# Attention on strips of the TensorE array: scores by row strips, values by column strips

## The chip, the cores and the metric

The kernel runs on one core of one Trainium2 chip. The metric is the device time of one execution in microseconds. Before the change three runs took 1524.38, 1525.86 and 1531.93 us; the median is 1525.86 us.

## What is computed

One layer over x of 4 x 2048 tokens with 512 features: a cross attention with 16 heads of 32 features over 77 context rows per batch, added to x, and then a mixture of 8 experts, top 2 of 8 with a capacity of 1024 tokens, added again.

```python
x = x + xattn(layernorm(x), ctx_768, Wq, bq, Wk, bk, Wv, bv, Wo, bo)
x = x + ffn(layernorm(x), expert_embeddings, first_linear, second_linear)

# xattn: heads H=16, D=32, scale D**-0.5
q = (query @ Wq + bq)        # [B, 16, 2048, 32]
k = (key_value @ Wk + bk)    # [B, 16, 77, 32]
v = (key_value @ Wv + bv)
attn = softmax(clip(einsum('bhqd,bhkd->bhqk', q, k) * scale, -1e4, 1e4))
x = einsum('bhqk,bhkd->bqhd', attn, v).reshape(B, Nq, Cq) @ Wo + bo

# ffn: router weights = softmax over the top 2 of 8 logits; each expert takes up to 1024 tokens
inter = relu(einsum('ech,eih->eci', tokens, first_linear))
out = einsum('eci,ehi->ech', inter, second_linear) * vals[:, :, None]
```

## The kernel before

The 8192 tokens are 64 tiles of 128. The kernel has two stages: attention with the router, and then the experts (from about 830 us on, not touched by the change). In attention the layernorm, scores, softmax and residual go tile by tile (index t); the query projection, the values product and their copies go by groups of two tiles (index G, 32 groups, 256 tokens, `GW` = 256).

Every product of the attention in 16 bits is made of three matmuls: operands are split into a high and a low half in fp16, and high x high, high x low and low x high are summed in PSUM. "g" is a head group of four heads, that is 128 of the 512 features.

The steps of the attention that the change and the prediction touch:

- `tx`, L601: PE transposes the normalised tile (fp32) into bank T; ACT copies the high half (L608), DVE makes the low half (L614).
- `q_mm`, L634: per G and g, 12 matmuls of 256 columns. ACT reads the bank twice (`halves`, L650): once as fp16 into `qT`, once as fp32 into `part`; POOL subtracts (`low`, L655) and gets the low half. `part` has four slots, which q and o share in turn.
- `s_mm`, L670: scores of tile t and head group g: 3 matmuls of 308 columns (4 heads x 77 keys). The stationary operand is q of 128 features x 128 tokens, and the keys stand block-diagonal in `kb`, three quarters of them zero. The four head groups have four PSUM banks, in two halves (S0, S1): a half is free once DVE has written `sd` from it.
- DVE per half: row maxima (`s_max`, L688 and L691), then subtraction into `sd` (`s_sub`, L695). ACT: Relu L703, Exp L707. DVE: sums L713. POOL normalises (L726), ACT casts (L731), POOL makes the low half (L735), and SP transposes both halves by DMA into `pT` (L740).
- `pv_mm`, L752: values, per G and g. The 16 x 77 = 1232 rows of keys lie in 10 chunks of 128. A head group touches 3 or 4 chunks; each is 3 matmuls of 128 x 128 against 256 columns, 39 in all per G. Each head group takes a PSUM bank of the pair A, uses 256 of its 512 columns, and is read by ACT twice (L651) and by POOL once (L655).
- `o_mm`, L773: output projection, 12 matmuls of 512 columns per tile. DVE adds the residual (L780). `t2`, L796: PE transposes the result, ACT copies it into `x1T` (L802, two buffers), `logits`, L827: 4 matmuls of 8 columns in fp32, each of which the trace shows as two.
- `put`, L1006 on POOL, `pick`, L991 on ACT and `invert`, L1017 on PE build the table of tokens per expert.

The banks A (two) serve `q_mm`, `pv_mm` and `o_mm` in turn. The order of instructions on each engine isn't the order of the code: a planner in the kernel keeps a clock per engine, and at each step takes the stage that can start in the earliest slot of 0.3 us by its table of costs, ties going by the table `RANK`. What stands in each engine's queue is fixed by that when the program is built; on the chip each engine works its queue in order and waits on semaphores.

Of the kernel before, what the change touches and what calls it, by code (L numbers as in the profile page):

```python
# [6 lines left out]
F32 = mybir.dt.float32  # L7
# [37 lines left out]
    "place1": 3.0, "values_max": 6.18, "values_split": 9.0, "values_place": 21.39, "output_max": 22.0,  # L45
    "output_split": 28.0, "factors": 9.28, "out_factor": 29.0, "keys_mm": -3.12, "keys_bias": -2.8,
    "values_mm": 4.1, "values_copy": 11.32, "emb_center": 20.48, "zero_v": -1.93, "numbers": 31.0,
    "ln1_stats": -6.54, "rsqrt1": 17.94, "ln1_apply": 18.24, "add_bo": 22.74, "tx": -4.11, "tx_hi": 26.0,
    "tx_lo": 19.9, "q_mm": 29.38, "q_hi": -27.75, "q_lo": 37.39, "s_mm": 47.47, "s_max": 82.86, "s_sum": 78.49,
    "p_norm": 80.36, "p_hi": 80.45, "p_lo": 24.82, "p_T": 105.11, "pv_mm": 101.04, "o_hi": 82.88, "o_lo": 72.54,  # L50
    "o_mm": 72.59, "residual": 94.24, "t2": 108.61, "t2_copy": 106.55, "logits": 130.25, "choose": 126.29,
    "choose2": 100.97, "rsqrt2": 83.51, "gates_of": 142.27, "rank": 156.16, "rank2": 141.44, "onehot": 194.91,
    "value": 184.83, "invert": 184.01, "load_w1": 300.0, "load_w2": 300.0, "prep": 400.0, "s_sub": 64.76,
    "s_min": 66.71, "s_exp": 72.85, "load_x": 70.23, "load_s": 12.21, "store_o": 84.42, "store_x": 74.15,
# [3 lines left out]
    "tx_lo": 0.65, "q_mm": 1.4, "q_hi": 0.87, "q_lo": 0.76, "s_mm": 0.42, "s_max": 0.45, "s_sub": 0.9, "s_min": 1.32, "s_exp": 1.32,  # L58
    "s_sum": 0.75, "p_norm": 2.28, "p_hi": 1.2, "p_lo": 2.5, "p_T": 2.8,
    "pv_mm": 1.15, "o_hi": 0.78, "o_lo": 0.76, "o_mm": 2.7, "residual": 0.0, "t2": 0.5, "t2_copy": 0.6,  # L60
# [90 lines left out]
def xattn_moe(nc, x, ctxT, wq, bq, wk, bk, wv, bv, wo, bo, embT, w1T, w2T, out, xrow):  # L151
    ctx = ExitStack()
    with ctx:
# [62 lines left out]
        part = sb("part", [P, 4, GW], F32)  # L216
# [3 lines left out]
        x1T = sb("x1T", [P, 2, 4, P], F32)  # L220
# [109 lines left out]
        dma("sp", lambda e: e.dma_start(wof[:, :, :], wo.rearrange("(c p) n -> p c n", p=P)), ("l_wo",))  # L330
# [149 lines left out]

        pieces = [(n, c, h, max(NKV * h, P * c), min(NKV * (h + 1), P * (c + 1))) for n, (g, c) in enumerate(PAIRS)
# [17 lines left out]
        def output_max():  # L499
            amax(3, flat3(wof[:, :, :]), [("l_wo",), ("s_z", 0)], ("a_o",))  # L500
            yield
            reduce_max(3, "sco", ("a_o",))
# [964 lines left out]
```

How the kernel before makes its waits and increments, by code:

```python
    def run(self, name, eng, sems):  # L141
        for item in self.queues[name]:
            if item[0] == "wait":
                eng.wait_ge(sems[item[1]], item[2])
            else:
                ins = item[1](eng)
                if item[2] is not None:
                    ins.then_inc(sems[item[2]], item[3])
```

## Time and profile before

| what | value |
| --- | --- |
| median of three runs | 1525.86 us |
| the profiled execution's own time | 1524.85 us |
| its span | 1523.1 us |
| PE busy | 1411.5 us |
| DVE busy | 982.1 us |
| POOL busy | 857.8 us |
| ACT busy | 825.6 us |
| `s_mm` (L670), matmuls, busy | 768, 129.7 us |
| `pv_mm` (L752), matmuls, busy | 1248, 161.5 us |

PE is TensorE's matmuls, PEld its weight loads, DVE is VectorE, ACT ScalarE, POOL GpSimd, SP the queue that issues most DMAs. The ends of matmuls are modelled: a matmul's length in the trace includes its way through the array, so that the next one starts before it ends. What a run of matmuls costs is read from the start of the run to the start of the next one.

### The profile page before, as it was taken

Reading aid. Unit: us, or ns where it says so; the run is one execution under the profiler, and the core shown is the slowest. Engines: PE = TensorE matmul, PEld = TensorE weight load, DVE = VectorE, ACT = ScalarE, POOL = GpSimd, SP = SyncE. Lnnn points to the kernel's source line nnn. Section 1 sums busy time; section 2 is a strip of 40 time slices with the busy share of each in tenths; the row PEclk is TensorE's granted clock in tenths of the full one; section 3 lists DMA queues with packets and bytes.
Section 4 is the critical chain, followed back from the end, with each engine's and each line's share of the span. In section 5 each row is a group of like instructions: output and inputs, shape, how many; then the busy total and the mean of one; then the engine's idle time right before and its main releaser. Section 6 shows DMA issues by size and latency. Waiting matters only on the chain.

```text
span 1523.1 us, 23892 instructions
## 1 busy us (share of the span) xinstructions
PE 1411.5 (93%) x8807; PEld 875.2 (57%) x8807; DVE 982.1 (64%) x1950; ACT 825.6 (54%) x1472; POOL 857.8 (56%) x907
## 2 busy tenths in 40 slices
PE   6787999989998999999964899999999999999996
PEld 2565777768776777768743644444444444444442
DVE  7895898978877877787766454545454555545430
ACT  4675787668886888768854451504233342425120
POOL 2596788879997899878966414232232414151301
PEclk9898999999999999999976999999999999999998
DMA  6166877568664655746734347465556556474401
GB/s 227 47 154 141 187 200 175 128 143 209 149 145 92 150 122 129 191 102 148 187 93 142 98 129 182 128 171 149 149 164 159 161 127 165 125 196 116 114 14 42
DMA packets 312062, 215.09 MB, mean 141 GB/s; under 512 B 252345, under 2 KB 252729, under 8 KB 311946
## 3 DMA queue, kind: packets, MB, share of 16 engines
q1 hardware_dynamic: 295411, 162.84, 43.6%
q0 software_dynamic: 15360, 50.66, 11.3%
q8 instruction: 70, 1.15, 0.3%
q14 instruction: 46, 0.38, 0.1%
q10 hardware_dynamic: 1175, 0.07, 0.1%
HBM read 105.62 MB, written 50.86 MB: 103 GB/s over the span
## 4 chain that ended last, share of the span: by engine, by line
PE 79%; DVE 5%; SPq 4%; POOL 4%; ACT 3%; issue 2%; DMA 2%; ACTq 1%; DVEq 0%; POOLq 0%
PE ps L1314 22%; PE ps L1335 22%; PE ps L634 9%; PE ps L773 7%; PE ps L752 7%; PE ps L670 5%; SPq L494 3%; PE ps L827 2%; PE ps L601 2%; POOL put L1006 1%; PE ps L796 1%; POOL ph L735 1%; DMA pT<-ph 1%; PE ps L464 1%; DMA wvf<-wv 1%
## 5 line engine op out<-in xcount | busy, mean ns | idle before, releaser
L1314 PE MATMUL ps<-xT,w1s 128*128 128x512 f16 (+1 forms) x1632 | 335.2, 368 | 0.0
L1335 PE MATMUL ps<-w2s,hT 128*128 128x512 f16 x1536 | 332.8, 379 | 0.0
L1320 ACT ACTIVATE hT<-ps 128x512 f16<-128x512 f32 (+1 forms) x136 | 77.8, 572 | 359.7 <-PE ps L1314 359.7
L1314 PEld LDWEIGHTS ps<-xT,w1s 128*128 128x128 f16 x1632 | 160.4, 98 | 172.3
L1335 PEld LDWEIGHTS ps<-w2s,hT 128*128 128x128 f16 x1536 | 150.2, 98 | 181.3
L1345 POOL DMA_INDIRECT out_dram<-ys,idx x64 | 71.7, 1120 | 277.6 <-DVE ys L1340 277.6
L634 PE MATMUL ps<-xnT,wqh 128*128 128x256 f16 x1536 | 189.4, 280 | 9.4 <-DVE xnT L614 7.5
L1322 DVE SCALAR_TENSOR_TENSOR hT<-ps,hT 128x512 f16<-128x512 f32 (+1 forms) x136 | 88.9, 658 | 140.6 <-ACT hT L1320 140.5
L735 POOL TENSOR_TENSOR ph<-sd,ph 128x1232 f16<-128x1232 f32 x64 | 161.9, 2530 | 30.6 <-ACT ph L731 30.5
L634 PEld LDWEIGHTS ps<-xnT,wqh 128*128 128x128 f16 x1536 | 153.6, 101 | 33.1 <-DVE xnT L614 9.0
L752 PE MATMUL ps<-pT,vb 128*128 128x256 f16 (+1 forms) x1248 | 161.5, 278 | 11.6 <-issue 10.3
L773 PE MATMUL ps<-woh,oT 128*128 128x512 f16 x768 | 171.0, 379 | 0.1
L1340 DVE SCALAR_TENSOR_TENSOR ys<-ps,gs,og 128x512 f32<-128x512 f32 x64 | 48.1, 751 | 189.0 <-PE ps L1335 189.0
L726 POOL TENSOR_TENSOR sd<-sd,rr 128x1232 f32<-128x1232 f32 x64 | 144.0, 2250 | 3.4 <-ACT rr L719 3.2
L752 PEld LDWEIGHTS ps<-pT,vb 128*128 128x128 f16 (+1 forms) x1248 | 123.9, 102 | 29.1 <-issue 12.4
L670 PE MATMUL ps<-kb,qT 128*128 128x308 f16 x768 | 129.7, 300 | 9.3 <-DVE sd L695 8.2
L688 DVE TENSOR_REDUCE ps<-ps 128x8 f32<-128x616 f32 x128 | 102.5, 800 | 47.4 <-PE ps L670 47.0
L773 PEld LDWEIGHTS ps<-woh,oT 128*128 128x128 f16 x768 | 74.4, 98 | 84.7 <-issue 0.4
L695 DVE SCALAR_TENSOR_TENSOR sd<-ps,lim,mx 128x616 f32<-128x616 f32 x128 | 108.7, 849 | 2.5
L713 DVE TENSOR_REDUCE sm<-sd 128x8 f32<-128x616 f32 x128 | 96.8, 778 | 18.0 <-ACT sd L707 18.0
L596 POOL TENSOR_TENSOR xt<-xt,bos 128x512 f32<-128x512 f32 x64 | 82.7, 1293 | 38.0 <-ACT xnf L590 30.3
L655 POOL TENSOR_TENSOR qT<-part,qT 128x256 f16<-128x256 f32 x128 | 85.2, 674 | 31.3 <-ACT part L650 31.2
(185 smaller groups left out, 2200.3 us busy)
## 6 DMA issues: line engine op xcount, KB each, us to landing
xs<-x SPq DMA_DIRECT2D x64, 256.0 KB, 2.9
xt<-x SPq DMA_DIRECT2D x64, 256.0 KB, 3.1
xrow_dram<-x SPq DMA_DIRECT2D x64, 256.0 KB, 3.3
out_dram<-x SPq DMA_DIRECT2D x64, 256.0 KB, 3.5
stage<-w1T SPq DMA_DIRECT2D x8, 2048.0 KB, 10.1
stage<-w2T SPq DMA_DIRECT2D x8, 2048.0 KB, 8.4
wqf<-wq SPq DMA_DIRECT2D x1, 1024.0 KB, 7.7
wof<-wo SPq DMA_DIRECT2D x1, 1024.0 KB, 11.8
```

What stands on the lines that cost most here:

```text
L634: do("pe", lambda e, k=k, a=a, b=b, i=i, last=last: e.matmul(bA[n][:, 0:GW], wqh[:, b, k, g * P:(g + 1) * P], xnT[:, G % 2, 4 * a + k, :], ...
L670: do("pe", lambda e, a=a, c=c, i=i: e.matmul(bS[g][:, 0:GK], qT[:, G % 2, a, g, j * P:(j + 1) * P], kbv(b, c)[:, g].rearrange("p j k -> p ...
L688: do("dve", lambda e: e.tensor_reduce(four(raw), scores(half), AX_X, ALU.max), after=[("s", t, 2 * half + 1)], mark=("raw", t, half))
L695: do("dve", lambda e: e.scalar_tensor_tensor(sd[:, t % SDB, 2 * GK * half:2 * GK * (half + 1)].rearrange("p (g j k) -> p g j k", g=2, j=4) ...
L713: do("dve", lambda e, hs=hs: e.tensor_reduce(sm[:, t % 2, hs], heads(t)[:, hs, :], AX_X, ALU.add), after=[("e", t)], mark=("sm", t, half))
L726: do("pool", lambda e: e.tensor_tensor(heads(t), heads(t), rr[:, t % 2, :].unsqueeze(2).to_broadcast([P, HEADS, NKV]), ALU.mult), after=[( ...
L735: do("pool", lambda e: e.tensor_tensor(ph[:, t % 2, 1, 0:KALL], sd[:, t % SDB, :], ph[:, t % 2, 0, 0:KALL], ALU.subtract), after=[("phi", ...
L752: do("pe", lambda e, k=k, c=c, a=a, d=d, K=K, i=i: e.matmul(bA[n][:, 0:GW], vb[0:K, b, a, k, :], pT[0:K, G % 2, d, c, :], start=(i == 0), ...
L773: do("pe", lambda e, g=g, a=a, b=b, i=i, last=last: e.matmul(bA[n][:, :], oT[:, G % 2, a, g, j * P:(j + 1) * P], woh[:, b, g, :], start=(g ...
L1314: do("pe", lambda q, k=k, a=a, b=b, i=i, last=last: q.matmul(hb[z][:, 0:wide], w1s[e % 2][:, a, k, ic * P:(ic + 1) * P], xT[:, 4 * b + k, ...
L1322: do("dve", lambda q: q.scalar_tensor_tensor(lo, hb[z][:, 0:wide], 0.0, hi, ALU.max, ALU.subtract), after=[("hhi", e, n, part)], mark=("hl ...
L1335: do("pe", lambda q, k=k, a=a, b=b, i=i, last=last: q.matmul(yb[z][:, :], hT[:, a, k, s * P:(s + 1) * P], w2s[e % 2][:, b, k, :], start=(k ...
```

## The change

Scores: each of the four heads of a group gets a strip of 32 rows of the array (`tile_position=(32*j, 0)`), with its own 32 features of q and its own 77 keys. A tile now has 48 matmuls of 77 columns instead of 12 of 308. Head j of each group writes to PSUM bank j, so that four consecutive matmuls address four strips and four banks. All 48 are one step, which waits for both halves of the banks; the maxima of the first half wait for the last of the 48.

Values: each head gets a strip of 32 columns of the array (`tile_position=(0, 32*j)`) and writes to 32 partitions of PSUM. A head's 77 rows lie in 1 or 2 chunks (25 pieces for 16 heads), each with three matmuls: 75 of 256 columns per G instead of 39. They are written in rounds over the four strips, 6 rounds per head group. Two head groups share one bank, each with 256 of its columns, so that ACT reads 512 columns at once and POOL subtracts 512 at once: 2 of each per G instead of 4.

Beside that: `part` with four slots becomes `partq` and `parto` with two slots each; `x1T` has one buffer instead of two, so that its copy waits for the logits of the tile before; the heads lie in a new order, which is undone by taking the rows of `wo` in that order (four DMAs instead of one) and the columns of the values likewise; `RANK` and `COST` have new numbers.

```diff
-    "tx_lo": 0.65, ..., "s_mm": 0.42, "s_max": 0.45, ...
+    "tx_lo": 0.65, ..., "s_mm": 0.62, "s_max": 0.45, ...
-    "pv_mm": 1.15, "o_hi": 0.78, "o_lo": 0.76, "o_mm": 2.7, ...
+    "pv_mm": 1.7, "o_hi": 1.2, "o_lo": 1.25, "o_mm": 2.7, ...
...
-        part = sb("part", [P, 4, GW], F32)
+        partq = sb("partq", [P, 2, GW], F32)
+        parto = sb("parto", [P, 2, 2 * GW], F32)
...
-        x1T = sb("x1T", [P, 2, 4, P], F32)
+        x1T = sb("x1T", [P, 4, P], F32)
...
-        dma("sp", lambda e: e.dma_start(wof[:, :, :], wo.rearrange("(c p) n -> p c n", p=P)), ("l_wo",))
+        wo_j = wo.rearrange("(j g d) n -> j d g n", j=4, g=4)
+        for j in range(4):
+            dma("sp", lambda e, j=j: e.dma_start(wof[DH * j:DH * (j + 1), :, :], wo_j[j]), ("l_wo", j), 0)
...
-        def s_mm(t, g):
-            G, j = divmod(t, TG)
-            b, half = t // TPB, g // 2
-            for i, (a, c) in enumerate(((0, 0), (0, 1), (1, 0))):
-                do("pe", lambda e, a=a, c=c, i=i: e.matmul(
-                    bS[g][:, 0:GK], qT[:, G % 2, a, g, j * P:(j + 1) * P],
-                    kbv(b, c)[:, g].rearrange("p j k -> p (j k)"), start=(i == 0), stop=(i == 2)),
-                   after=[("qlo", G, g), free[f"S{half}"] if g % 2 == 0 else None, ("kb0", 3), ("kb1", 3)],
-                   mark=("s", t, g) if i == 2 else None)
-            free[f"S{half}"] = ("cl", t, half)
+        def s_mm(t):
...
+            for g in range(4):
+                for i, (a, c) in enumerate(((0, 0), (0, 1), (1, 0))):
+                    for j in range(4):
+                        strip = slice(DH * j, DH * (j + 1))
+                        do("pe", lambda e, g=g, a=a, c=c, i=i, j=j, strip=strip: e.matmul(
+                            bS[j][:, NKV * g:NKV * (g + 1)], qT[strip, G % 2, a, g, tokens],
+                            kbv(b, c)[strip, g, j, :], start=(i == 0), stop=(i == 2), tile_position=(DH * j, 0)),
+                           after=[("qlo", G, g), free["S0"], free["S1"], ("kb0", 3), ("kb1", 3)],
+                           mark=("s", t, g) if i == 2 and j == 3 else None)
+            free["S0"], free["S1"] = ("cl", t, 0), ("cl", t, 1)
...
-               after=[("s", t, 2 * half + 1)], mark=("raw", t, half))
+               after=[("s", t, 3)], mark=("raw", t, half))
...
-        def pv_mm(G, g):
...
+        def pv_mm(G, half):
...
+            for g in (2 * half, 2 * half + 1):
+                cols = slice(GW * (g % 2), GW * (g % 2 + 1))
+                spans = [range(NKV * h // P, (NKV * (h + 1) - 1) // P + 1) for h in range(4 * g, 4 * g + 4)]
+                rounds = [(a, d, r) for r in range(max(len(w) for w in spans)) for a, d in ((0, 0), (0, 1), (1, 0))]
+                todo = [(j, spans[j][r], a, d) for a, d, r in rounds for j in range(4) if r < len(spans[j])]
...
+                    do("pe", lambda e, j=j, k=k, c=c, a=a, d=d, K=K, strip=strip, first=first, last=last, cols=cols:
+                       e.matmul(bA[n][strip, cols], vb[0:K, b, a, k, strip], pT[0:K, G % 2, d, c, :], start=first,
+                                stop=last, tile_position=(0, DH * j)),
+                       after=[("pT", TG * G + m) for m in range(TG)] + [was, vdm[b]],
+                       mark=("pv", G, half) if g % 2 and i == len(todo) - 1 else None)
+
+        def o_hi(G, half):
+            n = bank_of["pv", G, half]
+            halves(("o", G, half), o_both(G, 0, half), bA[n][:, :],
+                   [("pv", G, half), ("wo16", "lo"), back("o", TG * G + TG - 1, 2 * TG)])
...
-               after=[("t2", t), back("lg", t, 2)], mark=("x1T", t))
+               after=[("t2", t), back("lg", t, 1)], mark=("x1T", t))
```

The new numbers of the planner move the instructions. On PE, one group in the middle of the attention, from one output projection (`woh,oT`) to the next. Before, scores are `kb,qT` and values `pT,vb`; a number behind x is the count of matmuls in the row:

```order
L773 MATMUL ps<-woh,oT 128x512 x24
L796 MATMUL ps<-identf,x_89 128x128 x4
L752 MATMUL ps<-pT,vb 128x256 x9
L796 MATMUL ps<-identf,x_89 128x128 x4
L670 MATMUL ps<-kb,qT 128x308 x6
L827 MATMUL ps<-embc,x1T 128x8 x4
L752 MATMUL ps<-pT,vb 128x256 x9
L601 MATMUL ps<-identf,xnf 128x128 x4
L752 MATMUL ps<-pT,vb 128x256 x12
L827 MATMUL ps<-embc,x1T 128x8 x4
L601 MATMUL ps<-identf,xnf 128x128 x4
L634 MATMUL ps<-xnT,wqh 128x256 x24
```

The values of one G stand in four pieces with transposes, scores and logits between them. After, with lines moved (L680 scores, L773 values, L796 output projection, L819 second transpose, L850 logits, L1040 the token table, L605 first transpose, L638 queries), the end of such a group:

```order
L773 MATMUL ps<-pT,vb 32x256 x36
L819 MATMUL ps<-identf,x_90 128x128 x4
L773 MATMUL ps<-pT,vb 32x256 x39
L850 MATMUL ps<-embc,x1T 128x8 x4
L1040 MATMUL ps<-put,pick 128x64 x8
L605 MATMUL ps<-identf,xnf 128x128 x4
L850 MATMUL ps<-embc,x1T 128x8 x4
L796 MATMUL ps<-woh,oT 128x512 x24
L638 MATMUL ps<-xnT,wqh 128x256 x24
```

The values stand in two pieces of 36 and 39, and the output projection comes after 8 matmuls of the token table, one transpose and two logits.

On POOL the same part of the program, before: `ph` is the low half of the probabilities (1232 columns), `oT<-part` the low half of the values (256 columns), `xt` the addition of the bias, `sd<-sd,rr` the normalisation:

```order
L735 TENSOR_TENSOR ph<-sd,ph 128x1232
L1006 TENSOR_SCALAR put<-iota,colf,local 128x64 x2
L655 TENSOR_TENSOR oT<-part,oT 128x256
L1006 TENSOR_SCALAR put<-iota,colf,local 128x64 x2
L596 TENSOR_TENSOR xt<-xt,bos 128x512
L655 TENSOR_TENSOR oT<-part,oT 128x256
L726 TENSOR_TENSOR sd<-sd,rr 128x1232
L655 TENSOR_TENSOR oT<-part,oT 128x256
L596 TENSOR_TENSOR xt<-xt,bos 128x512
L735 TENSOR_TENSOR ph<-sd,ph 128x1232
```

After, `oT<-parto` has 512 columns:

```order
L745 TENSOR_TENSOR ph<-sd,ph 128x1232
L660 TENSOR_TENSOR oT<-parto,oT 128x512
L600 TENSOR_TENSOR xt<-xt,bos 128x512
L660 TENSOR_TENSOR oT<-parto,oT 128x512
L736 TENSOR_TENSOR sd<-sd,rr 128x1232
L600 TENSOR_TENSOR xt<-xt,bos 128x512
L1029 TENSOR_SCALAR put<-iota,colf,local 128x64 x2
L745 TENSOR_TENSOR ph<-sd,ph 128x1232
```

There are two `oT` per G instead of four, each twice as wide, and the second one is directly ahead of the next normalisation.

## Rows read from the trace of the kernel before

**Rows 1.** The page: busy time (us, share, instructions) and the chain by engine

```profile
PE 1411.5 (93%) x8807; PEld 875.2 (57%) x8807; DVE 982.1 (64%) x1950; ACT 825.6 (54%) x1472; POOL 857.8 (56%) x907
...
PE 79%; DVE 5%; SPq 4%; POOL 4%; ACT 3%; issue 2%; DMA 2%; ACTq 1%; DVEq 0%; POOLq 0%
```

**Rows 2.** Stretches, us from the start: length, busy us per engine, granted clock, DMA share

```profile
100.00:800.00 700.00, 657.75 (x5108) 506.83 (x5106) 554.40 (x1197) 526.50 (x1011) 580.01 (x609) 0.96 0.63 150
200.00:400.00 200.00, 193.31 (x1503) 150.65 (x1502) 173.11 (x375) 153.00 (x287) 166.69 (x173) 0.97 0.69 167
400.00:600.00 200.00, 193.41 (x1531) 149.72 (x1529) 154.75 (x324) 161.22 (x316) 178.71 (x189) 0.98 0.57 133
445.68:467.29 21.61, 21.59 (x180) 16.85 (x178) 17.87 (x47) 18.62 (x37) 21.16 (x31) 1.00 0.75 161
800.00:840.00 40.00, 17.71 (x122) 11.76 (x119) 23.77 (x96) 17.67 (x43) 25.99 (x39) 0.66 0.42 135
```

**Rows 3.** Timeline of PE (start, length, line): first and last output projection run

```profile
99.84 5.34 PE L773 MATMUL ps<-woh,oT 128*128 128x512 f16 x24
...
800.91 5.34 PE L773 MATMUL ps<-woh,oT 128*128 128x512 f16 x24
```

**Rows 4.** Timeline of PE, one group of two tiles, 445 to 467 us

```profile
445.68 5.34 PE L773 MATMUL ps<-woh,oT 128*128 128x512 f16 x24
...
451.30 1.15 PE L752 MATMUL ps<-pT,vb 128*128 128x256 f16 x9
452.28 0.56 PE L670 MATMUL ps<-kb,qT 128*128 128x308 f16 x3
...
453.50 0.95 PE L827 MATMUL ps<-embc,x1T 128*128 128x8 f32 x8
...
456.52 1.47 PE L752 MATMUL ps<-pT,vb 128*128 128x256 f16 x12
457.83 0.95 PE L670 MATMUL ps<-kb,qT 128*128 128x308 f16 x6
458.61 0.60 PE L601 MATMUL ps<-identf,xnf 128*128 128x128 f32 x4
...
467.17 0.28 PE L1017 MATMUL ps<-put,pick 128*128 128x64 f16 x4
467.29 5.34 PE L773 MATMUL ps<-woh,oT 128*128 128x512 f16 x24
```

**Rows 5.** The page's groups of PE matmuls and of DVE on the scores

```profile
L752 PE MATMUL ps<-pT,vb 128*128 128x256 f16 (+1 forms) x1248 | 161.5, 278 | 11.6 <-issue 10.3
...
L670 PE MATMUL ps<-kb,qT 128*128 128x308 f16 x768 | 129.7, 300 | 9.3 <-DVE sd L695 8.2
L688 DVE TENSOR_REDUCE ps<-ps 128x8 f32<-128x616 f32 x128 | 102.5, 800 | 47.4 <-PE ps L670 47.0
...
L695 DVE SCALAR_TENSOR_TENSOR sd<-ps,lim,mx 128x616 f32<-128x616 f32 x128 | 108.7, 849 | 2.5
```

**Rows 6.** Groups of DVE, POOL and ACT, 400 to 600 us

```profile
L691 DVE TENSOR_SCALAR mx<-ps,lim 128x8 f32<-128x8 f32 x37 | 10.3, 279 | 0.8
...
L735 POOL TENSOR_TENSOR ph<-sd,ph 128x1232 f16<-128x1232 f32 x19 | 48.1, 2534 | 4.0 <-ACT ph L731 4.0
L726 POOL TENSOR_TENSOR sd<-sd,rr 128x1232 f32<-128x1232 f32 x18 | 40.5, 2248 | 0.2 <-ACT rr L719 0.2
L655 POOL TENSOR_TENSOR oT<-part,oT 128x256 f16<-128x256 f32 x36 | 24.2, 675 | 1.4 <-ACT part L651 1.3
...
L596 POOL TENSOR_TENSOR xt<-xt,bos 128x512 f32<-128x512 f32 x17 | 21.6, 1271 | 5.0 <-ACT xnf L590 4.9
...
L651 ACT COPY part<-ps 128x256 f32<-128x256 f32 x36 | 13.9, 386 | 0.0
...
L802 ACT COPY x1T<-ps 128x512 f32<-128x512 f32 x18 | 10.7, 594 | 5.9 <-PE ps L796 5.9
```

**Rows 7.** Waits, 100 to 800 us: who waited for whom, us, times, longest

```profile
DVE ps L688 <- PE ps L670: 45.8, 44, 3.6
```

More of the change, by code:

```diff
@@ L742, in p_T @@
                 ph[:, t % 2].rearrange("p a n -> p (a n)")), ("pT", t), t % 2,
-                after=[("plo", t), ("pz", 1 if t else 0), back("pv", G, 2, 3)])
-        def pv_mm(G, g):
+                after=[("plo", t), ("pz", 1 if t else 0), back("pv", G, 2, 1)])
+        def pv_mm(G, half):
             b = G * TG // TPB
-            n, was = take("A", ("pv", G, g))
-            free[f"A{n}"] = ("of", G, g)
-            todo = [(k, c, a, d) for k, (gg, c) in enumerate(PAIRS) if gg == g for a, d in ((0, 0), (0, 1), (1, 0))]
-            for i, (k, c, a, d) in enumerate(todo):
-                K = min(P, KALL - c * P)
-                do("pe", lambda e, k=k, c=c, a=a, d=d, K=K, i=i: e.matmul(
-                    bA[n][:, 0:GW], vb[0:K, b, a, k, :], pT[0:K, G % 2, d, c, :],
-                    start=(i == 0), stop=(i == len(todo) - 1)),
-                   after=[("pT", TG * G + j) for j in range(TG)] + [was, vdm[b]],
-                   mark=("pv", G, g) if i == len(todo) - 1 else None)
@@ L758, in o_hi @@
-        def o_hi(G, g):
-            n = bank_of["pv", G, g]
-            halves(("o", G, g), oT[:, G % 2, 0, g, :], bA[n][:, 0:GW],
-                   [("pv", G, g), ("wo16", "lo"), back("o", TG * G + TG - 1, 2 * TG)])
-        def o_lo(G, g):
-            low(("o", G, g), oT[:, G % 2, 0, g, :], oT[:, G % 2, 1, g, :])
+            n, was = take("A", ("pv", G, half))
+            free[f"A{n}"] = ("of", G, half)
+            for g in (2 * half, 2 * half + 1):
[3 more added lines that the diff above has]
+                todo = [(j, spans[j][r], a, d) for a, d, r in rounds for j in range(4) if r < len(spans[j])]
+                ends = {j: max(n for n, piece in enumerate(todo) if piece[0] == j) for j in range(4)}
+                begins = {j: min(n for n, piece in enumerate(todo) if piece[0] == j) for j in range(4)}
+                for i, (j, c, a, d) in enumerate(todo):
+                    k = PAIRS.index((g, c))
+                    K = min(P, KALL - c * P)
+                    strip = slice(DH * j, DH * (j + 1))
+                    first, last = i == begins[j], i == ends[j]
+                    do("pe", lambda e, j=j, k=k, c=c, a=a, d=d, K=K, strip=strip, first=first, last=last, cols=cols:
[3 more added lines that the diff above has]
+                       mark=("pv", G, half) if g % 2 and i == len(todo) - 1 else None)
@@ L775, in o_mm @@
                         start=(g == 0 and i == 0), stop=last),
-                       after=[("olo", G, g), was, ("wo16", "lo")], mark=("o", t) if last else None)
+                       after=[("olo", G, g // 2), was, ("wo16", "lo")], mark=("o", t) if last else None)
         def residual(t):
```

65 lines of the change are left out of this document (37 added, 28 removed).

## The prediction

> **What bounds the kernel now.** I read the page's busy times and its chain first: PE is busy 93% of the span and holds 79% of the chain that ended last, and no other engine holds over 5% [rows 1]. The stretches come next, because a share over the whole span mixes the attention with the experts, which the change doesn't touch. From 100 to 800 us PE is busy 657.8 of 700 us, POOL 580.0, DVE 554.4 and ACT 526.5 [rows 2]. So the attention hangs on PE too, but POOL is only 12% behind it, and from 400 to 600 us, where the token table is also built, only 8% (178.7 against 193.4). What PE can give back ends there.
>
> The timeline gives the period. The first output projection starts at 99.84 us and the last of the 32 at 800.91 [rows 3]: 31 periods of 22.6 us, one for each group G of two tiles. An undisturbed one goes from 445.68 to 467.29 us and is 21.6 us long, with PE busy for all of it [rows 2, 4]. So 1.0 us of a period is waiting and disturbance, and 21.6 us is what PE needs for its work. POOL needs 580.0 / 31 = 18.7 us per period on average, 178.7 / 9 = 19.9 between 400 and 600 us (at 22.2 us, 9 periods fit in 200 us), and 21.2 in the one just named. DVE needs 17.9 on average and some 19.2 between 200 and 400 us, ACT 17.0 [rows 2].
>
> **What the two products cost PE now.** A matmul's mean length (300 ns for scores, 278 for values [rows 5]) contains its way through the array; the price is the distance between starts. Nine matmuls of the values start at 451.30 and the scores follow at 452.28: 109 ns each; twelve from 456.52 to 457.83 give 109 again [rows 4]. Six of the scores from 457.83 to 458.61 are 130 ns each [rows 4]. Per G, then, scores take 24 x 0.130 = 3.1 us and values 39 x 0.109 = 4.25 us. The other PE work stays as it is: 21.6 - 3.1 - 4.25 = 14.25 us.
>
> **Scores after.** 96 matmuls of 77 columns per G. At the rate of the row (130 / 308 = 0.42 ns per column) one is 32.5 ns. If the four strips work side by side it is 24 rounds x 32.5 = 0.8 us; if they go one after another, 96 x 32.5 = 3.1 us, as much as today, because the block-diagonal form wastes exactly what the strips save. That a small matmul with its own weights doesn't cost more than its columns is seen on the token table: four of 64 columns from 467.17 to 467.29 start 30 ns apart [rows 4], 0.47 ns per column. So scores can hardly get dearer, and lie between 0.8 and 3.1 us. No row shows strips. Consecutive matmuls address different rows, different banks and different operands, so nothing in the code ties them; I take 1.2, nearer to the low end, with half as much again for issue.
>
> **Values after.** 75 matmuls of 256 columns per G. Side by side: 4 head groups x 6 rounds x 0.109 = 2.6 us. One after another: 75 x 0.109 = 8.2 us, nearly twice today's 4.25, for here each matmul keeps all 256 columns and fills only a quarter of the array. This is the term that decides the sign. I take 3.3, a quarter over the low end: the second round of each head group has only two or three strips at work, and four moving streams must be fed at once.
>
> The Trainium skill (TensorE: Matmul & The Clock Gate, Measured speedup vs the span model) gives 3.07 times for four row strips and 2.38 times for three column strips of 512 columns. An estimate by that page: 2.38 of 3 is 79%, so the values would take 2.6 / 0.79 = 3.3 us, and the scores at 77% about 1.0. No run here shows it yet. The same page says that column strips give up the fast weight load, and that a load then takes its columns divided by 1.2 GHz; by that, an estimate, 75 loads of 32 columns would be 2.0 us per G, beside the matmuls and below them. In the trace a load is 99 ns in the mean (875.2 us for 8807 [rows 1]) and lies beside the matmuls.
>
> **Changing form.** Per G there are two blocks of scores and two of values, so up to 8 changes between strips and whole array. If at each the array empties first, it costs what a matmul is long beyond its distance, 278 - 109 = 169 ns [rows 4, 5], 1.35 us in all; if not, nothing. I take the middle, 0.7. The Trainium skill (TensorEngine Tiling (Array Packing), Key Properties) says that a change of the tiling mode drains TensorE; by it the sum would be 0.65 us per G higher on PE, which stays under the bound that I come to.
>
> PE's need is then 14.25 + 1.2 + 3.3 + 0.7 = 19.4 us.
>
> **ACT, POOL, DVE.** ACT reads 512 columns in 594 ns where it read 256 in 386 [rows 6]: per G 4 reads for 8, 2.4 us for 3.1, a gain of 0.7 that nobody waits for. POOL subtracts 512 in about 1.27 us (the addition of the bias has that width) where it took 4 x 0.675 = 2.7 [rows 6]: 2.54, a gain of 0.16. So POOL needs 19.7 us in the part with the token table. DVE does the same work. All of its waiting on scores (45.8 us in 44 waits [rows 7]) sat behind PE.
>
> **Period after.** PE 19.4, POOL 18.5 on average and 19.7 in the dense part, DVE up to 19.2: three engines within 5%. One bound engine cost 1.0 us over its need per period; with three close together I allow 1.4 over 19.4, so 20.8 us. That is 1.8 us less, times 31: 56 us.
>
> **What is added.** (1) The scores of a tile now wait for both halves of the banks. The loop is 48 matmuls (0.6 to 1.6 us), then DVE twice 0.800 + 0.279 + 0.849 = 3.9 us [rows 5, 6]; at most 5.5 us against 10.4 per tile, hidden, provided that DVE's queue doesn't hold it back. (2) The output projection waits for POOL's second `oT`. From the end of the values that is two ACT reads (1.2) and POOL's 1.27, 2.5 us. In the order after, PE has the logits of two tiles (0.8 us each), a transpose of 0.4 and 8 matmuls of the table (0.24), 2.3 us, to do meanwhile [rows 4]. So it fits barely, and if POOL is just in `ph` (2.53 us [rows 6]) PE stands for as much. On PE's queue behind it are queries and transposes, which DVE and ACT need. (3) `partq` has two slots: ACT's second copy waits for POOL two head groups back, and the queries' bank is released behind it. Price from 0 to one `ph` per G. (4) `x1T` with one buffer: the copy waits for logits which stand several rows earlier in PE's queue; nothing. (5) Three more DMAs at the start, about 1.5 us of SP's queue, in a part where PE waits for other things; 0 to 1.5 us. (1) to (5) are inside the allowance of 1.4 unless (2) or (3) bites.
>
> The other order of the first 100 us and the last 30 of the attention I put at nothing, give or take 5 us: there the setup and the token table set the time, not the two products. The profiled execution took 1524.85 us, 1.0 under the median shown. 1524.85 - 56 = 1469, so 1470 on the scale of the median.
>
> **The rivals.**
>
> *A, the strips don't work side by side (slower).* Mechanism: the column strips of the values share what feeds the array, so that matmuls which should overlap follow each other. PE is the bound already, and all of it shows. It decides from where scores, values and changes together pass today's 7.35 us. Two values at a time with serial scores: 38 x 0.109 + 3.1 + 1.35 = 8.6, PE needs 22.9, period 23.9, +1.3 x 31 = +40 us: 1566. All serial: 3.1 + 8.2 + 1.35 = 12.65, period 27.9, +164 us: 1690. For it: no row here shows two matmuls at once. Against: loads and matmuls already overlap, and the strips have banks or partitions of their own.
>
> *B, the gain turns into waits of PE on ACT and POOL.* (2) and (3) cost one `ph`, 2.5 us per G, at the output projection or the queries: 19.4 + 2.5 = 21.9, with some of the allowance 22 to 22.6. That is 0 to 18 us saved: 1507 to 1526. For it: POOL is busy 21.2 of 21.6 us in the undisturbed period. Against: on average it has 4 us free.
>
> *C, the ideal.* PE 14.25 + 0.8 + 2.6 + 0.6 = 18.25, POOL 18.5 as the bound on average, 1.0 over it: 19.5, 3.1 x 31 = 96 us less: 1430. Against: POOL's own dense part at 19.7, and an order that can't fill three engines at 95%.
>
> The clock is not a case of its own: it is 0.97 from 200 to 400 us with PE busy 97%, and 0.66 from 800 to 840 us where PE is busy 44% [rows 2]. At 90% busy or more I expect 0.95 and above. If it fell to the lower level of 1.2 GHz in a tenth of the time, it would cost about 2 us per period at worst, and this is in the range.
>
> **Chances.** The forecast, 1450 to 1490: 0.50. C: 0.12. B: 0.18, of which 0.08 is faster by over 0.5%, 0.08 within and 0.02 slower (0.5%, some 7.6 us, is about what a measurement of this kernel can tell from no change). A: 0.20. So faster 0.70, same 0.08, slower 0.22. Range 1430 to 1545: it reaches to C and through B, and leaves out most of A.
>
> **What would show it.** The output projections would stand about 20.8 us apart. Scores: a block of 48 is 0.4 to 0.8 us long from start to next start (0.6 chosen; 1.6 would be serial). Values: 75 in about 3.3 us (8.2 serial). PE's busy share from 100 us to the end of the attention goes down, POOL's up to 90% or more; the wait of DVE L688 on scores shrinks. Experts: no change. I am wrong if the 75 take over 5 us, or if PE stands over 2 us before each output projection.

## The result, and the profile after

Twenty runs of each kernel: 1531.97 us after, 1526.45 before. The ratio is 1.0033, with a 95% interval from 1.0022 to 1.0044. The change makes the kernel slower by a third of a per cent, about 5 us, where 56 us less were forecast. The profiled execution has a span of 1530.8 us (1523.1 before).

First the page: busy times and the chain, then five groups (busy us, mean ns | idle before, who ended it). L680 are the scores, L773 the values, L638 the queries, L796 the output projection, L605 the first transpose.

```profile
PE 1353.8 (88%) x12263; PEld 800.7 (52%) x12263; DVE 981.3 (64%) x1950; ACT 816.2 (53%) x1344; POOL 845.8 (55%) x843
...
PE 64%; POOL 10%; DVE 9%; ACT 6%; SPq 4%; issue 4%; DMA 3%; ACTq 0%; POOLq 0%; DVEq 0%
...
L638 PE MATMUL ps<-xnT,wqh 128*128 128x256 f16 x1536 | 201.9, 291 | 15.5 <-DVE xnT L618 9.9
L796 PE MATMUL ps<-woh,oT 128*128 128x512 f16 x768 | 188.7, 404 | 13.9 <-POOL oT L660 13.7
...
L773 PE MATMUL ps<-pT,vb 128*32 128x256 f16 (+1 forms) x2400 | 92.5, 292 | 11.0 <-issue 5.6
...
L680 PE MATMUL ps<-kb,qT 32*128 32x77 f16 x3072 | 42.2, 201 | 12.7 <-DVE sd L705 8.1 <-POOL qT L660 3.9 <-issue 0.3
...
L605 PE MATMUL ps<-identf,xnf 128*128 128x128 f32 x256 | 47.6, 317 | 50.0 <-ACT x1T L825 27.3 <-DVE xnT L618 14.0 <-ACT xnf L594 8.2
```

The queries (L634 there), the output projection (L773 there) and the first transpose (L601) of the kernel before, for comparison:

```profile
L634 PE MATMUL ps<-xnT,wqh 128*128 128x256 f16 x1536 | 189.4, 280 | 9.4 <-DVE xnT L614 7.5 <-ACT part L650 1.6 <-ACT part L651 0.3
L773 PE MATMUL ps<-woh,oT 128*128 128x512 f16 x768 | 171.0, 379 | 0.1
...
L601 PE MATMUL ps<-identf,xnf 128*128 128x128 f32 x256 | 42.4, 292 | 18.1 <-DVE xnT L614 9.5 <-ACT xnf L590 8.2 <-ACT x1T L802 0.3
```

The strips do what was hoped, and more: 2400 matmuls of the values are busy for 92.5 us where 1248 took 161.5, and the scores 42.2 where they took 129.7 [rows 5]. But PE as a whole is busy only 58 us less, and its idle time (span less busy) goes from 111.6 to 177.0 us, up by 65. These two make the 8 us by which the span is longer. Half of the added idle time, 32 us, stands before the first transposes (18.1 before, 50.0 after), which wait most for ACT to take the T bank's last content away. The output projection, which hardly ever waited (0.1 us), now waits 13.9. PE's share of the chain falls from 79% to 64%, POOL's rises from 4% to 10%, DVE's from 5% to 9% [rows 1]: the gain has turned into waiting.

The stretches (us per engine, granted clock, DMA share):

```profile
200.00:400.00 200.00, 172.91 (x2382) 125.03 (x2380) 164.59 (x365) 147.03 (x253) 159.88 (x153) 0.88 0.67 163
400.00:600.00 200.00, 178.70 (x2502) 130.60 (x2503) 158.43 (x327) 160.46 (x282) 177.18 (x173) 0.91 0.62 133
600.00:800.00 200.00, 161.23 (x2290) 114.76 (x2289) 154.59 (x367) 148.29 (x260) 160.31 (x157) 0.90 0.58 139
800.00:840.00 40.00, 21.20 (x125) 14.04 (x123) 24.04 (x90) 12.10 (x29) 23.21 (x33) 0.67 0.41 139
100.00:800.00 700.00, 595.73 (x8317) 429.79 (x8303) 553.96 (x1206) 524.24 (x902) 574.43 (x549) 0.90 0.64 149
```

From 100 to 800 us PE is busy 595.7 us for 657.8 [rows 2], and POOL, DVE and ACT do in the same 700 us what they did before, within 1%. The granted clock is 0.90 for 0.96. So matmuls that the change didn't touch got longer: queries 291 ns in the mean (280 before, by the group of L634), output projections 404 (379), which is 12.5 and 17.7 us more of busy time in these two groups.

The timeline of PE shows what single blocks cost (start, length, line):

```profile
446.44 1.49 PE L638 MATMUL ps<-xnT,wqh 128*128 128x256 f16 x12
447.85 1.49 PE L773 MATMUL ps<-pT,vb 128*32 128x256 f16 x39
449.43 1.48 PE L638 MATMUL ps<-xnT,wqh 128*128 128x256 f16 x12
...
457.24 0.60 PE L680 MATMUL ps<-kb,qT 32*128 32x77 f16 x48
457.77 1.18 PE L773 MATMUL ps<-pT,vb 128*32 128x256 f16 x36
458.88 0.66 PE L819 MATMUL ps<-identf,x 128*128 128x128 f32 x4
459.46 1.49 PE L773 MATMUL ps<-pT,vb 128*32 128x256 f16 x39
460.88 1.06 PE L850 MATMUL ps<-embc,x1T 128*128 128x8 f32 x8
462.76 0.63 PE L605 MATMUL ps<-identf,xnf 128*128 128x128 f32 x4 [0.82 <-ACT x1T L825]
463.22 1.37 PE L850 MATMUL ps<-embc,x1T 128*128 128x8 f32 x8
464.45 6.59 PE L796 MATMUL ps<-woh,oT 128*128 128x512 f16 x24
470.88 0.60 PE L605 MATMUL ps<-identf,xnf 128*128 128x128 f32 x4
```

A block of 48 scores takes 0.53 us (457.24 to 457.77), the values 1.11 and 1.42 us (457.77 to 458.88, 459.46 to 460.88): 2.5 us per group for 4.25 [rows 4]. Going into strips costs 0.10 to 0.14 us: the twelve queries at 446.44, with strips behind them, take 1.41 us and not 1.31, the four transposes at 458.88 take 0.58 and not 0.44. Whole-array matmuls pay this when strips follow them. The same twelve queries take 1.32 us where whole-array matmuls follow (449.43 to 450.75), and the 48 scores take 0.53 or 0.54 us whether strips or whole-array matmuls come next. The output projection at 464.45 takes 6.43 us until the next start, at a granted clock of 0.80 in this stretch; at 1.00 it takes 5.18 (445.68 to 450.86 us in the kernel before). Part of it ran at the lower level of 1.2 GHz.

In the kernel before, 22 of the 31 steps between output projections are 20 to 24 us long. After, long and short steps alternate for much of the attention; the first six are 23.5, 33.1, 12.8, 24.3, 12.9 and 34.0 us. The second and third:

```profile
124.80 5.35 PE L796 MATMUL ps<-woh,oT 128*128 128x512 f16 x24 [0.49 <-POOL oT L660]
...
132.50 0.96 PE L850 MATMUL ps<-embc,x1T 128*128 128x8 f32 x8
141.91 1.09 PE L605 MATMUL ps<-identf,xnf 128*128 128x128 f32 x4 [8.45 <-ACT x1T L825]
...
146.52 4.28 PE L638 MATMUL ps<-xnT,wqh 128*128 128x256 f16 x24
...
157.93 5.56 PE L796 MATMUL ps<-woh,oT 128*128 128x512 f16 x24
...
170.68 1.67 PE L796 MATMUL ps<-woh,oT 128*128 128x512 f16 x7
```

33.1 us, then 12.8. The short step isn't a group's own time: it has none of the 48 queries that each group needs. The two together are 45.9 us, 22.9 per group. Inside the long one PE stands for 8.45 us, and the 24 queries after it take 4.21 us (granted clock 0.64) where they take 2.62 at full clock. ACT and SP show why it stands:

```profile
131.31 0.58 ACT L825 COPY x1T<-ps 128x512 f32<-128x512 f32 x1 [1.27 <-PE ps L819]
140.48 0.81 ACT L594 ACTIVATE xnf<-xt,mv 128x512 f32<-128x512 f32 x1 [8.59 <-DMA xt<-x]
...
119.94 17.54 SPq L498 DMA_DIRECT2D vb<-vsh  x20
137.52 0.51 SPq L315 DMA_DIRECT2D xt<-x  x1
```

ACT waits 8.59 us for a tile of x, and with it the T bank, PE's transposes and the scores. The load of that tile stands in SP's queue behind 20 DMAs that place values, 0.88 us each. Before, the longest such row had 11.

### The profile page after: what moved, and what is told of

Same layout as the page of the kernel before. It is cut to its first block, busy times and chain, and to the rows that moved or that the text cites. A ratio compares the mean times of both kernels' runs of the same rounds, so it can differ in the third digit from the quotient of the medians.

```text
span 1530.8 us, 30592 instructions
## 1 busy us (share of the span) xinstructions
PE 1353.8 (88%) x12263; PEld 800.7 (52%) x12263; DVE 981.3 (64%) x1950; ACT 816.2 (53%) x1344; POOL 845.8 (55%) x843
## 4 chain that ended last, share of the span: by engine, by line
PE 64%; POOL 10%; DVE 9%; ACT 6%; SPq 4%; issue 4%; DMA 3%; ACTq 0%; POOLq 0%; DVEq 0%
PE ps L1337 22%; PE ps L1358 22%; PE ps L796 7%; PE ps L638 6%; POOL ph L745 3%; SPq L498 3%; POOL sd L736 2%; POOL put L1029 2%; PE ps L605 2%; PE ps L773 1%; POOL oT L660 1%; PE ps L850 1%; DVE sd L705 1%; DMA xt<-x 1%; DVE sm L723 1%
## 5 line engine op out<-in xcount | busy, mean ns | idle before, releaser
L638 PE MATMUL ps<-xnT,wqh 128*128 128x256 f16 x1536 | 201.9, 291 | 15.5 <-DVE xnT L618 9.9
L796 PE MATMUL ps<-woh,oT 128*128 128x512 f16 x768 | 188.7, 404 | 13.9 <-POOL oT L660 13.7
L638 PEld LDWEIGHTS ps<-xnT,wqh 128*128 128x128 f16 x1536 | 157.4, 105 | 48.6 <-DVE xnT L618 10.8
L796 PEld LDWEIGHTS ps<-woh,oT 128*128 128x128 f16 x768 | 77.5, 104 | 113.5 <-POOL oT L660 21.2
L660 POOL TENSOR_TENSOR qT<-partq,qT 128x256 f16<-128x256 f32 x128 | 85.4, 674 | 52.8 <-ACT partq L655 52.4
L773 PE MATMUL ps<-pT,vb 128*32 128x256 f16 (+1 forms) x2400 | 92.5, 292 | 11.0 <-issue 5.6
L605 PE MATMUL ps<-identf,xnf 128*128 128x128 f32 x256 | 47.6, 317 | 50.0 <-ACT x1T L825 27.3
L1077 POOL PARTITION_ALL_REDUCE scr<-scr x16 | 5.7, 355 | 155.2 <-DVE scr L1073 143.2
```

The costliest lines, as they stand in the source:

```text
L638: do("pe", lambda e, k=k, a=a, b=b, i=i, last=last: e.matmul(bA[n][:, 0:GW], wqh[:, b, k, g * P:(g + 1) * P], xnT[:, G % 2, 4 * a + k, :], ...
L660: do("pool", lambda e: e.tensor_tensor(lo, copy, hi, ALU.subtract), after=[(key[0] + "f", *key[1:])], mark=(key[0] + "lo", *key[1:]))
L773: e.matmul(bA[n][strip, cols], vb[0:K, b, a, k, strip], pT[0:K, G % 2, d, c, :], start=first, stop=last, tile_position=(0, DH * j)),
L796: do("pe", lambda e, g=g, a=a, b=b, i=i, last=last: e.matmul(bA[n][:, :], oT[:, G % 2, a, g, j * P:(j + 1) * P], woh[:, b, g, :], start=(g ...
```

## The experiments

Each kernel ran on the same chip as the kernel before; times are medians, ratios are to the kernel before with their 95% interval. Two experiments may have run on different chips, and then their ratios are the fair comparison. "The same order" means that every engine's queue holds the same instructions in the same places.

### The strips in one order: e1_whole and e3_twice

```diff
 # e1_whole, on the changed kernel
-   for j in range(4): e.matmul(bS[j][:, NKV * g:NKV * (g + 1)], qT[strip, ...], ..., tile_position=(DH * j, 0))
+   e.matmul(bS[g][:, 0:GK], qT[:, G % 2, a, g, tokens], kbv(b, c)[:, g].rearrange("p j k -> p (j k)"), ...)
-   e.matmul(bA[n][strip, cols], vb[0:K, b, a, k, strip], pT[0:K, G % 2, d, c, :], ..., tile_position=(0, DH * j))
+   e.matmul(bA[n][:, cols], vb[0:K, b, a, k, :], pT[0:K, G % 2, d, c, :], ...)
 # e3_twice, on the changed kernel
-   for j in range(4):
+   for j, rep in [(j, rep) for rep in range(2) for j in range(4)]:      # the values: each matmul twice in a row
```

> The changed kernel with every instruction in the same place of its queue, the same waits, buffers and copies, but with the scores and values back in whole-array form (12 matmuls of 308 columns per tile, 39 of 256 per group). PE's need per group goes from about 17.9 us (14.25 + 1.06 + 2.6, as the blocks of the changed kernel stand in its trace) back to 21.6. Theory 1, the strips' time on PE no longer matters because the order in the queues and the waits set the period: 1530 to 1550 us. Theory 2, PE sets the period in this order too and the strips really save 3.7 us per group, which something else in the new order has eaten: 1532 + 31 x 3.7 = about 1645, at least 1600.

> The changed kernel with each of the strip matmuls issued twice (scores and values are doubled thereby), order and waits the same. PE gets about 3.7 us more per group. Theory 1, PE has that much slack and its waits shrink, and its granted clock rises from 0.90 to 0.94 or more: 1530 to 1550. Theory 2, PE at its lowered clock is the bound: 1532 + 31 x 3.7 = about 1640.

Measured: e1_whole 1586.25 us (1.0378, from 1.033 to 1.0426); e3_twice 1626.89 us (1.0635, from 1.0583 to 1.0688). e1_whole lies between the theories. The strips are worth 1586 - 1532 = 54 us in this order, half of the 31 x 3.7 = 115 that PE saves. And the new order with all that goes with it costs 1586 - 1526.5 = 60 us, with the matmuls of before. That is the whole account: +60 - 54 = +6. It is the account of one path: the order was planned with the costs of strips, and the whole-array matmuls that stand in it here are longer, so some of the 60 us may come from that mismatch.

e3_twice adds every product twice, so its scores and values are doubled; only its time counts. It is 95 us longer than the changed kernel, nearer to theory 2: PE has no slack for the added matmuls, though it is idle 15% of the time from 100 to 800 us. But the 95 us aren't the price of PE time alone. The doubled blocks take 0.96 us for 0.53 and 2.53 and 2.73 for 1.11 and 1.42, 3.6 us more per group; e1_whole adds as much (3.8, less some 0.4 for going into strips) and costs 54. Of the other 41 us, 21 show as idle time of PE before the values with no wait that the profile shows, 24.2 us in all for 3.6 in e1_whole:

```profile
L774 PE MATMUL ps<-pT,vb 128*32 128x256 f16 (+1 forms) x4800 | 186.5, 287 | 27.0 <-issue 24.2
```

The rest stays open.

### The values alone: e2_values

```diff
 # on the kernel before: 4 column strips, one bank per head group as before
-   e.matmul(bA[n][:, 0:GW], vb[0:K, b, a, k, :], pT[0:K, G % 2, d, c, :], ...)
+   e.matmul(bA[n][strip, 0:GW], vb[0:K, b, a, k, strip], pT[0:K, G % 2, d, c, :], ..., tile_position=(0, DH * j))
```

> The kernel before, with nothing changed but the 39 matmuls of the values per group, which become 75 on column strips; order of the queues, four banks per group and all copies as before. In the changed kernel the 75 took 2.6 us instead of 4.25. Theory 1, PE was the bound and the strips alone give their time: 1526 - 31 x 1.65 = 1475. Theory 2, another engine or the fixed order stands right behind PE, and PE's clock falls when it waits: 1505 to 1526.

Measured 1515.3 us (0.9926, from 0.9899 to 0.9952): a gain, but 11 of 51 us. Theory 2. PE's busy time from 100 to 800 us falls by 7.6 us only: more groups fit in the stretch, and the clock is 0.95 for 0.96; POOL is now busy 588.5 of the 700 us.

```profile
100.00:800.00 700.00, 650.12 (x6283) 463.84 (x6276) 560.38 (x1214) 533.22 (x1029) 588.46 (x624) 0.95 0.65 151
```

### SP's bursts: e4_after_noplace and e5_before_noplace

```diff
 # Plan.dma, in both kernels
+        if mark[0] == "l_vb" and slot:
+            self.at[mark] = self.at[("l_vb", 24)]
+            return
```

> The changed kernel without the 75 small DMAs that place the values of batches 1 to 3 (their values stay zero); everything else stands in the same order. In the changed kernel 20 of them stand in a row on SP's queue from 119.9 to 137.5 us, 0.88 us each, and the load of an x tile behind them holds ACT for 8.6 us and PE for 8.4. Theory 1, these bursts ahead of the x loads are what ate the gain: 1495 to 1512, PE's longest waits gone. Theory 2, they cost their one or two visible waits and no more: 1518 to 1526. Theory 3, the time is made up for later: 1529 to 1533.

> The kernel before, without the 75 small DMAs that place the values of batches 1 to 3 (these values stay zero); order the same. The changed kernel gained 14 us from the same cut. Theory 1, SP's bursts are a cost that the change made worse (20 in a row against 11): this one gains only 3 to 7 us, 1519 to 1523. Theory 2, they cost both kernels the same: 1510 to 1515, and they explain nothing of the difference.

Measured: 1517.89 us (0.9944, from 0.9918 to 0.997) and 1512.2 us (0.99, from 0.9867 to 0.9934). Without these DMAs (the values of batches 1 to 3 stay zero) either kernel is 14 us faster, give or take 5. The burst, the most striking wait of the trace after, costs the old kernel as much and doesn't explain the missing 56 us.

### The order table and the buffers: e6_old_rank and e8_buffers

```diff
 # e6_old_rank, on the changed kernel: RANK of the kernel before
-    "q_mm": 40.85, ... "s_mm": 58.94, ... "pv_mm": 114.71, ... "o_mm": 86.26, ...
+    "q_mm": 29.38, ... "s_mm": 47.47, ... "pv_mm": 101.04, ... "o_mm": 72.59, ...
 # e8_buffers, on the changed kernel, same order
-        kb = sb("kb", [P, B, 2, 4, 4 * NKV], F16)
+        kb = sb("kb", [P, B, 2, 4, NKV], F16)
-        partq = sb("partq", [P, 2, GW], F32); parto = sb("parto", [P, 2, 2 * GW], F32); x1T = sb("x1T", [P, 4, P], F32)
+        partq = sb("partq", [P, 4, GW], F32); parto = sb("parto", [P, 4, 2 * GW], F32); x1T = sb("x1T", [P, 2, 4, P], F32)
```

> The changed kernel with the planner's RANK table of the kernel before; strips, wide copies, buffers and the planner's new costs stay. Theory 1, the new order table is what cost the 60 us which the whole-array form showed in the new order: 1480 to 1510. Theory 2, it is the structure (one step for the scores of a tile, that waits for both halves of the banks and for all of q; values and copies in two pieces per group instead of four), and the table only makes the best of it: 1535 to 1560.

> The changed kernel in exactly its order, with two buffers of x1T and four slots each for partq and parto (room from a key table that holds only the blocks that are not zero; its memset at the start is a quarter as long). Theory 1, the waits on these small buffers (ACT x1T on the logits 6.9 us, oT and partq copies on POOL) are part of where the gain went: 1515 to 1525. Theory 2, they cost nothing beside the others, since POOL and PE are late anyway: 1529 to 1534.

Measured: 1547.93 us (1.0138, from 1.0096 to 1.018) for the old table, 1529.52 us (1.0012, from 0.9989 to 1.0036) for the buffers. So the new table is no culprit, it had won 16 us back, and the narrow buffers cost 2 us, within the noise. Theory 2 both times.

### The scores alone, and what their block costs: e7_scores, e12_scores_whole, e13_fine_waits

```diff
 # e7_scores, on the kernel before; its RANK, rings, x1T and values stay; the heads lie in the new order
-    "s_mm": 0.42        # COST, four steps per tile
+    "s_mm": 0.62        # COST, one step per tile
-        def s_mm(t, g):            # 4 steps per tile
+        def s_mm(t):               # 1 step, 48 matmuls on row strips, waits for S0 and S1
 # e12_scores_whole, on e7_scores, same order
-                    for j in range(4): e.matmul(bS[j][:, NKV * g:NKV * (g + 1)], qT[strip, ...], ...)
+                    e.matmul(bS[g][:, 0:GK], qT[:, G % 2, a, g, tokens], ...)
 # e13_fine_waits, on e12_scores_whole, same order: the left-out keys count in the planner only
-   after=[("qlo", G, g), free["S0"], free["S1"], ...]      # scores
+   after=[("qlo", G, g), free["S0"], Soft(free["S1"]) if g < 2 else free["S1"], ...]
-   after=[("s", t, 3)]                                     # maxima of each half
+   after=[("s", t, 2 * half + 1), Soft(("s", t, 3))]
```

> The kernel before with the scores alone on row strips (48 matmuls in one step per tile, heads in the new order), and its own RANK table, rings, x1T and values. Strips save 2 x (1.57 - 0.53) = 2.1 us of PE per group. Theory 1, PE bound: 1526 - 65 = about 1461. Theory 2, as one step that waits for both halves they make PE stand behind DVE's scores and shorten nothing: 1525 to 1560.

> The kernel with the scores alone in one step per tile (1558 us with row strips), the order the same, but the scores in whole-array form: 12 matmuls of 308 columns. It has only the grouping of the scores, not the strips. Theory 1, strips save their 2.1 us of PE per group and the grouping costs more than that: 1600 to 1625, 75 to 100 over the kernel before. Theory 2, strips save little here because PE waits anyway: 1560 to 1580; then the grouping costs 35 to 55.

> The whole-array scores in one block per tile (1588 us), every instruction in the same place of its queue, but with the waits of the kernel before: the first half of the block waits only for its own two banks, and DVE's first maxima only for the first half of the block. Theory 1, the coarse waits cost the 61 us (DVE stands for the whole block, PE for both halves): 1530 to 1550. Theory 2, it is where the block stands in the order: 1575 to 1590.

Measured: e7_scores 1558.5 us (1.0216, from 1.0171 to 1.0261), e12_scores_whole 1587.73 us (1.0395, from 1.0357 to 1.0433), e13_fine_waits 1579.38 us (1.0371, from 1.0328 to 1.0414). e12_scores_whole fell between its two theories. With the matmuls and RANK of before, putting a tile's scores into one step costs 61 us, the same as the whole new order did in e1_whole; strips give 29 back. The wait of DVE on the scores, 100 to 800 us, in e12_scores_whole and then e13_fine_waits (45.8 us before [rows 7]):

```profile
DVE ps L694 <- PE ps L676: 89.9, 37, 9.2
...
DVE ps L699 <- PE ps L680: 72.7, 28, 10.3
```

It doubles. By the ratios, fine waits take back 4 of the 61 us, and the two intervals overlap, so it isn't shown that they take back any. So it isn't the semaphores as such: with the waits of before, in this order, the kernel is still 3.7% slower. What is left is the order, and why the order is bad was not tested. I think that it is where the planner puts a block that can't start before both halves and all four head groups of q are ready: it comes later in PE's queue and in lumps, and everything queued behind it moves with it. A second cause isn't excluded: the table gives the one step 0.62 us, the cost of the strips, where the 12 whole-array matmuls take 1.57 us and the kernel before had 4 x 0.42 = 1.68 in it. So e12_scores_whole and e13_fine_waits, like e1_whole, run an order planned for shorter blocks, and part of the 61 us can come from that. No run has the one step with its true cost. e7_scores, whose cost in the table fits its strips (0.53 us), is still 33 us slower than the kernel before (from 26 to 40) while it saves 2 us of PE per group, so the one step costs time without this mismatch too.

### New orders: e9_values_order, e11_whole_in_e9_order, e10_after_order, e16_before_order, e14_all, e15_all_longer

For these RANK and some of COST were searched: for each trial the planner was run, and the queues that it made were replayed with the durations of the traces (0.86 us for a DMA that places values) and with PE at half speed after a long gap, as in the 24 queries after the gap of 8.45 us above. The replay only chose the order; the times are the chip's.

```diff
 # e9_values_order, on e2_values (numbers rounded, four of some eighty)
-    "s_mm": 47.47, "pv_mm": 101.04, "o_mm": 72.59, ... "values_place": 21.39
+    "s_mm": 39.98, "pv_mm": 96.83, "o_mm": 92.3, ... "values_place": 33.72
 # e11_whole_in_e9_order: the same table on the kernel before. e10_after_order: a table of its own on the changed kernel.
 # e16_before_order: a table of its own on the kernel before
 # e14_all, on the changed kernel, with the larger buffers of e8_buffers (parto 3 slots)
-    "q_mm": 40.85, "s_mm": 58.94, "o_mm": 86.26, ... "values_place": 19.46
+    "q_mm": 60.43, "s_mm": 71.99, "o_mm": 132.75, ... "values_place": 26.89
 # e15_all_longer: the same, searched longer
```

> The kernel before with the values on column strips (as in the run that had only those) and an order planned anew: the planner's RANK and COST hold other numbers, with the costs on PE and on SP's queue as the traces have them (0.86 us for a DMA that places values, where the table said 0.5). Theory 1, what held the gain back was the order of the queues, which must be planned for the shorter blocks and for SP's real cost: 1475 to 1500. Theory 2, POOL and ACT stand so close behind PE that no order helps: 1505 to 1520.

> The control of the run with the new order: the same order in every queue, but the values in whole-array form, 39 matmuls per group. Theory 1, the strips are worth their PE time (1.65 us per group) where the order uses it: 25 to 45 us slower than the strips in the same order. Theory 2, the order alone makes the gain: within 12 us of them, as in the old order (11 us).

> The changed kernel, all of it, with RANK and COST planned anew in the same way. Theory 1, its order was the trouble and can be mended: 1500 to 1515. Theory 2, one step for the scores and pieces of two head groups make PE stand in any order: 1520 to 1540.

> The whole change (scores and values by strips, wide copies) with two buffers of x1T, four partq and three parto slots, and an order planned anew for longer. Theory 1, buffers and order together make the full change pay: 1500 to 1520. Theory 2, the scores as one step hold it back in any order, and it stays behind the values alone (1505): 1520 to 1540.

> The whole change with the larger buffers (as in e14_all, 1498.5 us) and an order planned still longer. Theory 1, the whole change is limited by its order alone and goes on gaining: 1480 to 1493. Theory 2, the waits of PE and its lowered clock hold it near what it has: 1495 to 1505.

> The kernel before, unchanged but for RANK and COST planned anew in the same way: what a new order is worth without any strip. Theory 1, the order alone gives little where PE is really busy 94% of the attention: 1518 to 1528. Theory 2, it gives as much as in the kernels with strips: 1495 to 1510, and the strips aren't needed for it.

| kernel | matmuls | median us | ratio | interval |
| --- | --- | --- | --- | --- |
| e16_before_order | whole | 1527.51 | 1.0005 | 0.9989 to 1.0021 |
| e11_whole_in_e9_order | whole | 1526.93 | 1.001 | 0.9988 to 1.0033 |
| e9_values_order | values on strips | 1504.68 | 0.9854 | 0.9827 to 0.9881 |
| e10_after_order | all strips, small buffers | 1536.62 | 1.0073 | 1.0044 to 1.0102 |
| e14_all | all strips, larger buffers | 1498.51 | 0.9851 | 0.9797 to 0.9905 |
| e15_all_longer | all strips, larger buffers | 1499.31 | 0.9814 | 0.9787 to 0.9841 |

Without strips neither of two other orders is worth anything. With strips of the values a new order is worth 11 us more than the old one: in that order they give 22 us, not 11. This lies between the theories of e11_whole_in_e9_order, and it is still less than half of the 51 us of PE time that they save. The whole change gains 23 and 28 us in its best two orders, by the ratios; their intervals run from 14 to 33. So with the order planned again, the scores on strips with all that comes with them add, by the ratios, between nothing and some 6 us to what the values alone give (22).

e10_after_order was a miss: expected at 1500 to 1515, it came out 5 us over the changed kernel, so the replay isn't a measurement. Whether e14_all owes its gain over e10_after_order to the buffers or to a better search isn't separated. At 1498.5 us it is faster than both of its theories said, and e9_values_order, at 1504.7, lies on the border between its own two. e15_all_longer refutes its own theory 1. Its times and those of e14_all can't be told apart.

e14_all against the changed kernel, 100 to 800 us: the same clock, PE's busy time the same within 3 us, and 13 us more of POOL's work done in the stretch:

```profile
100.00:800.00 700.00, 598.32 (x8386) 434.22 (x8384) 565.34 (x1284) 530.69 (x922) 587.82 (x569) 0.90 0.64 154
```

## Why the prediction was wrong

**The bound before: right.** PE needed its 21.6 us per group; e16_before_order and e11_whole_in_e9_order show that neither of two other orders gets under 1526.

**Scores, 1.2 us per group: 1.1 measured.** 0.53 us per block, within the range given for it and near its low end, so rival A was wrong. Serial strips were the wrong worry.

**Values, 3.3 us: 2.5 measured**, below the 2.6 that I had as the low end. A round with two strips may let the next one start in the free ones; that wasn't tested. The estimate from the Trainium skill's factors (TensorE: Matmul & The Clock Gate, Measured speedup vs the span model) was 3.3 and, for the scores, 1.0; the trace agrees with the second and beats the first.

**Changing form, 0.7 us:** 0.10 to 0.14 us was seen each time strips follow whole-array matmuls and nothing at the other changes, and a group has some three such places: 0.4 us. PE's need is then 14.25 + 1.1 + 2.5 + 0.4, some 18.2 us at full clock. I said 19.4. Everything on PE was as good as forecast or better.

**The period, 20.8 us, is the step that failed.** I wrote "with three close together I allow 1.4 over 19.4". From the first output projection of the changed kernel (101.27 us) to the last (some 803 us) it is 22.6 us per group, 4.4 over PE's need and no shorter than before. PE is busy 595.7 / 31 = 19.2 us of it, at a clock of 0.90, and idle for 3.4. The allowance was a number beside a sum, taken from one kernel whose order was matched to its blocks. Nothing in it depended on the order that the change brought, and that order cost 60 us (e1_whole).

**"What is added" (1), the one block of scores: priced at nothing.** I compared the length of its loop (5.5 us) with the time per tile and called it hidden. e12_scores_whole prices it at 61 us, of which a part can be the planner's too small cost for the whole-array form. The loop was hidden; what it did to the order of the queues was not. (2), a part of rival B, shows in the waits (PE on POOL's `oT` before L796, 13.7 us in the run). (3) and (4), the narrow buffers, e8_buffers puts at 2 us, within the noise. That (4) costs nothing was right, though ACT's copy of `x1T` heads the wait before the first transposes.

**Rival B, the gain turned into waits of PE, is the nearest, but didn't come true as written.** It forecast 1507 to 1526, and the measured 1532 lies beyond its end. Its mechanism, 2.5 us per group at the output projection or the queries, is 13.9 and 15.5 us in the whole run, 0.9 per group together; half of the added idle time stands before the first transposes. Its 0.18 was too little all the same: POOL 21.2 of 21.6 us busy in an undisturbed period, and DVE at 19.2, were the rows that spoke for it.

**The signs of being wrong missed.** I named two: values over 5 us, and PE standing over 2 us before each output projection. They are 2.5 us and, in the mean, 0.4. The sign that would have caught it is the spacing of the output projections, which I gave as 20.8 us.

**The clock.** I expected 0.95 and above at 90% busy; PE was busy 85% and the clock was 0.90. Waits cost twice: the unchanged queries and output projections took 30 us more of busy time. That is a good part of why PE is busy only 58 us less, where the strips save 32 x 3.7 = 118. In the prediction the clock was "not a case of its own".

## What to carry to other kernels

Before a faster form of a block is priced by what it saves on its engine, ask what it does to the size of the step: a form that merges four steps into one, with the union of their waits, has to be priced as a change of the queue, by running the old instructions in the new order. Plan that order with the costs of the instructions that will stand in it, or the price is mixed with the mismatch. Here, with three engines 12 to 20% behind the bound and fixed queues, a saving on the bound engine came through to half or less: 54 of 115 us in one order, 11 of 51 in another, and 22 of 51 even with the order planned again for it. And the wait that catches the eye in the new trace may cost the old kernel just as much, so test it in both.

## What the runs showed of the hardware

- Four row strips of 32 rows run side by side: 48 matmuls of 77 columns with 48 loads of weights in 0.53 us, 11 ns each; a round of four takes 44 ns where 77 columns alone would be 32.5 ns by the rate of the kernel before.
- Column strips of 32 columns reach 31 ns per matmul of 256 columns (36 in 1.11 us), 3.5 times the rate of 109 ns. In the other block, 39 in 1.42 us, it is 36 ns.
- A block of whole-array matmuls takes 0.10 to 0.14 us longer when strips follow it; when strips end, no added time was visible.
- The granted clock over the span was 0.97 before (PE busy 93%), 0.93 after (88%) and 0.94 in e3_twice (90%): in these three it goes with PE's busy share.
